# Attention and feed-forward block on one core: columns as operands, two operations on another engine, quarter loads together, another order

## What is computed

```python
x = x + _L0_xattn_ref(_layernorm(x), ctx, Wq, bq, Wk, bk)   # softmax((ctx Wq')(ctx Wk')'), mixes the 256 columns of x
x = x + _L0_ffn_ref(_layernorm(x), w_norm, w_gv, w_out)     # RMS norm, 8-bit rows, ternary weights, value * silu(gate)
...
x = x + _L1_xattn_ref(_layernorm(x), ctx, mask, Wq, Wk, Wv, Wo)   # 16 heads of 128, 8 key/value heads
x = x + _L1_ffn_ref(_layernorm(x), gate_w, up_w, down_w, scales)  # weights rounded to float8, silu(gate) * up
...
```

## Time and profile before

| | us |
|---|---|
| three timed runs | 310.63, 313.87, 313.88 |
| their median | 313.87 |
| the profiled execution | 312.58 |
| its span, first to last instruction | 310.5 |
| TensorE busy in the span | 293.6 |
| VectorE busy | 260.9 |
| ScalarE busy | 253.7 |
| GpSimd busy | 218.5 |

### The profile page before, as it was taken

How to read it: one execution, slowest core, us unless ns; L and a number is a source line. 1 busy time by engine, 2 the same in 40 slices (tenths; PEclk the granted TensorE clock), 3 DMA queues, 4 the chain that set the end, 5 groups by cost and what they waited for, 6 DMA issues and landing times.

```text
span 310.5 us, 6396 instructions
## 1 busy us (share of the span) xinstructions
PE 293.6 (95%) x1980; PEld 259.9 (84%) x1992; DVE 260.9 (84%) x713; ACT 253.7 (82%) x603; POOL 218.5 (70%) x290
## 2 busy tenths in 40 slices
PE   3968999999999999999999999999999999999994
PEld 2755487798989998979889999999988999899884
DVE  3959999999999999889999986997768897675665
ACT  2398995598999998979999899778899999855460
POOL 3558864556998578999879998886678798952001
PEclk9979999999999999999999999999999999999999
DMA  7996032001326548885878756537645647200103
GB/s 223 367 381 199 35 101 70 1 8 30 93 47 189 157 138 251 220 212 139 228 210 226 199 144 174 161 108 219 182 144 148 179 143 211 68 3 0 36 1 101
DMA packets 54609, 44.59 MB, mean 144 GB/s; under 512 B 11696, under 2 KB 45104, under 8 KB 54576
## 3 DMA queue, kind: packets, MB, share of 16 engines
q1 hardware_dynamic: 54016, 43.93, 49.0%
q10 hardware_dynamic: 560, 0.26, 0.3%
HBM read 27.01 MB, written 15.20 MB: 136 GB/s over the span
## 4 chain that ended last, share of the span: by engine, by line
PE 59%; DVE 20%; DMA 8%; issue 5%; SPq 4%; ACT 2%; DVEq 0%
PE pb L2016 41%; DMA block_room<-blocks 5%; PE pb L2279 5%; PE pb L2314 4%; DMA wraw<-in_wgvT 3%; DVE blocks L1581 3%; SPq L442 2%; DVE sm L1564 2%; PE pb L2130 2%; PE pb L2091 2%; PE pb L2076 2%; DVE wraw L1455 2%; DVE step L1601 1%; PE pb L2227 1%; DVE q_lo L1551 1%
## 5 line engine op out<-in xcount | busy, mean ns | idle before, releaser
L667 POOL TENSOR_TENSOR tp_lo<-tp,pT_hi 128x512 fp32r<-128x512 f32 x54 | 70.0, 1311 | 15.1 <-ACT pT_hi L993 14.8
L981 ACT ACTIVATE sm<-sm,smin 128x256 f32<-128x256 f32 x128 | 63.6, 501 | 4.7 <-DVE smin L1564 4.4
L1564 DVE CUSTOM_DVE_ANT_0 sm<-pb,mask_all 128x256 f32<-128x256 f32 x128 | 47.3, 418 | 5.6 <-PE pb L2016 5.5
L1581 DVE STREAM_TRANSPOSE blocks<-sm 128x1024 f32<-128x1024 f32 x27 | 33.5, 1240 | 7.4 <-DMA block_room<-blocks 7.0
L2016 PE MATMUL pb<-ctx_hi,q_hi 128*128 128x256 f32 x128 | 38.1, 298 | 1.1 <-DVE q_lo L1551 0.6
L662 POOL TENSOR_SCALAR sm<-sm,srec 128x256 f32<-128x256 f32 x64 | 30.5, 488 | 10.4 <-DVE srec L1570 10.4
L2016 PE MATMUL pb<-xT_hi,m_hi 128*128 128x256 f32 x128 | 37.3, 292 | 0.3 <-DVE xT_lo L1540 0.3
L2016 PE MATMUL pb<-n_hi,oT_hi 128*128 128x256 f32 x128 | 37.1, 290 | 0.2 <-DVE oT_lo L1595 0.2
L2016 PE MATMUL pb<-xT_hi,m_lo 128*128 128x256 f32 x128 | 36.2, 283 | 0.0
L2016 PE MATMUL pb<-xT_lo,m_hi 128*128 128x256 f32 x128 | 36.2, 283 | 0.0
L2016 PE MATMUL pb<-ctx_lo,q_hi 128*128 128x256 f32 x128 | 36.2, 282 | 0.0
(11 more groups left out here) (195 smaller groups left out, 943.0 us busy)
## 6 DMA issues: line engine op xcount, KB each, us to landing
block_room<-blocks SPq DMA_DIRECT2D x108, 128.0 KB, 2.8
tp<-block_room SPq DMA_DIRECT2D x54, 256.0 KB, 3.0
w_raw<-in_w SPq DMA_DIRECT2D x4, 576.0 KB, 4.6
wraw<-in_wgvT SPq DMA_DIRECT2D x4, 512.0 KB, 8.4
wraw<-in_woutT SPq DMA_DIRECT2D x2, 512.0 KB, 9.3
out<-xb SPq DMA_DIRECT2D x4, 256.0 KB, 2.2
xa<-in_x SPq DMA_DIRECT2D x3, 256.0 KB, 4.5
xb<-in_ctxT SPq DMA_DIRECT2D x2, 256.0 KB, 5.1
```

The source lines that it names most:

```text
L667: g.tensor_tensor(tp_lo[:, z, c, :], tp[:, z, c, :], as_f32(pT_hi[:, c, :]), ALU.subtract).then_inc(pT_lo_pool, 1)
L981: a.activation(sm[:, n % 2, k, :], sm[:, n % 2, k, :], ACT.Exp, bias=smin[:, n % 2, k:k + 1], scale=-1.0, accum_out=ssum[:, n % 2, k:k + 1 ...
L1564: v.tensor_tensor_reduce(out=sm[:, n % 2, k, :], in0=bank(passing_bank("s", 2 * n + h))[:, (k % 2) * S:(k % 2 + 1) * S], in1=mask_all[:, b ...
L1581: v.transpose(blocks[:].rearrange("p g k b -> p k g b"), sm[:, n % 2, :, :].rearrange("p k (g b) -> p k g b", b=32)).then_inc(blocks_done, 1)
```

## The change

1. GpSimd fills four columns of constants at the start (`minus_one`, `least`, `over_one`, `per_127`), and `nmean`, `ve` and `hstep` read them in place of numbers in the instruction. `hmax` and `hqs`, before one operation of two tensors each, are now one operation for each tile, with the deviation `rstd` as a column. VectorE's first statistics and GpSimd's first rows wait for 8 fills in place of 4.
2. `context_low` and the mask's values are GpSimd's. The mask's last column is no longer a maximum over the mask's bytes but a comparison of the first row minimum of each batch, made by VectorE in step n = 1, 9, 17 and 25, and `added3` waits for it.
3. The context's first half is the first load and its second half the sixth; the output weights' first piece goes behind the gate and value weights; `eighth(1)` to `eighth(3)` go out close behind `eighth(0)`.
4. `PASSING`, the banks of the sums, and the lists of calls of all five engines are new. What is computed of products is the same.

```diff
+        minus_one = tile(ctx, "minus_one", [P, 1])
+        least = tile(ctx, "least", [P, 1])
+        over_one = tile(ctx, "over_one", [P, 1])
+        per_127 = tile(ctx, "per_127", [P, 1])
...
+        SUMS, DOWN = 5, ((7, 4), (6, 5))
...
@@ -460,52 +464,54 @@
                     sp.wait_ge(fused_vo_ps, PAIRS)
                     sp.wait_ge(x1_done, B)
                     sp.wait_ge(wmean_done, 2)
-                    sp.wait_ge(mask_step, 2)
+                    sp.wait_ge(mask_step, 1)
                 four = slice(B * n * PIECE, B * (n + 1) * PIECE)
                 sp.dma_start(w8_raw[:, four], w8[:, four]).then_inc(ld_eight[n], 16)
 
+            contexts(0)
             projection(1)
             projection(0)
-            contexts(0)
             rows(1)
             rows(2)
+            contexts(1)
             rows(3)
             gate_value(0)
-            contexts(1)
             gate_value(2)
-            hidden_out(0)
             gate_value(1)
             gate_value(3)
+            hidden_out(0)
             hidden_out(1)
             raw(0)
...
             raw(3)
-            scales()
+            mask_bytes()
             raw(8)
             raw(2)
             turn_rows(1)
             raw(9)
-            mask_bytes()
             raw(7)
-            turn_rows(2)
             eighth(0)
             turn_hidden(2)
+            turn_rows(2)
+            eighth(1)
+            eighth(2)
             turn_hidden(3)
+            eighth(3)
             blocks_written(3)
-            turn_rows(3)
             blocks_read(3)
             blocks_written(4)
+            turn_rows(3)
             blocks_read(4)
             blocks_written(5)
             blocks_read(5)
             blocks_written(6)
             blocks_read(6)
             blocks_written(7)
-            eighth(1)
             blocks_read(7)
...
@@ -572,6 +576,10 @@
             g = nc.gpsimd
             g.memset(identf[:], 0.0).then_inc(ident_zero, 1)
             g.memset(nhalf[:], -0.5).then_inc(filled, 1)
+            g.memset(minus_one[:], -1.0).then_inc(filled, 1)
+            g.memset(least[:], EPS).then_inc(filled, 1)
+            g.memset(over_one[:], 1.0 + EPS).then_inc(filled, 1)
+            g.memset(per_127[:], 1.0 / 127.0).then_inc(filled, 1)
...
             def rows1(b):
                 if b == 0:
-                    pool.wait_ge(filled, 4)
+                    pool.wait_ge(filled, 8)
                 power(slice(0, 1), b, ve1_done, rstd1_done)
                 if b >= 2:
                     pool.wait_ge(xnT_ps, b - 1)
                 rows(xn[:, b % 2, :, :], xa, b, xn1_done)
+
+            def context_low(n):
+                pool.wait_ge(ctx_hi_done, n + 1)
+                g.tensor_tensor(ctx_lo[:, ctx_part(n)], ctx_raw[:, ctx_part(n)], as_f32(ctx_hi[:, ctx_part(n)]), ALU.subtract).then_inc(ctx_lo_done, 1)
+
+            def mask_values():
+                pool.wait_ge(ld_mask, 16)
+                g.tensor_scalar(mask_all[:, 0:B, 0:S], mask8[:], -MASKED, MASKED, ALU.mult, ALU.add).then_inc(mask_step, 1)
...
@@ -1386,10 +1405,6 @@
             v.memset(onesf[:], 1.0).then_inc(filled, 1)
             v.memset(plus_round[:], ROUND)
             v.memset(minus_round[:], -ROUND).then_inc(filled, 1)
-
-            def context_low(n):
-                dve.wait_ge(ctx_hi_done, n + 1)
-                v.tensor_tensor(ctx_lo[:, ctx_part(n)], ctx_raw[:, ctx_part(n)], as_f32(ctx_hi[:, ctx_part(n)]), ALU.subtract).then_inc(ctx_lo_done, 1)
 
             def values_low(c):
                 dve.wait_ge(cr_hi_done, c + 1)
@@ -1407,12 +1422,14 @@
                 for t in range(sl.start, sl.stop):
                     v.bn_aggr(mv[:, t, :], bnst[:, t, :]).then_inc(mv_done, 1)
                 dve.wait_ge(mv_done, bn_count[0])
-                v.tensor_scalar(nmean[:, sl], mv[:, sl, 0], -1.0, None, ALU.mult)
+                v.tensor_scalar(nmean[:, sl], mv[:, sl, 0], minus_one[:, 0:1], None, ALU.mult)
 
             def variances(sl, done):
-                v.tensor_scalar(ve[:, 0, sl], mv[:, sl, 1], EPS, None, ALU.add).then_inc(done, 1)
+                v.tensor_scalar(ve[:, 0, sl], mv[:, sl, 1], least[:, 0:1], None, ALU.add).then_inc(done, 1)
...
             def stats1(b):
+                if b == 0:
+                    dve.wait_ge(filled, 8)
...
-                v.tensor_scalar(ve[:, 0, sl], mv[:, sl, 1], EPS, None, ALU.add)
-                v.tensor_scalar(ve[:, 1, sl], mv[:, sl, 1], 1.0 + EPS, EPS * EPS, ALU.mult, ALU.add).then_inc(ve2_done, 1)
+                v.tensor_scalar(ve[:, 0, sl], mv[:, sl, 1], least[:, 0:1], None, ALU.add)
+                v.tensor_scalar(ve[:, 1, sl], mv[:, sl, 1], over_one[:, 0:1], EPS * EPS, ALU.mult, ALU.add).then_inc(ve2_done, 1)
...
-                scale_next(v.tensor_tensor(hmax[:, sl], hmax[:, sl], rstd[:, 1, sl], ALU.mult))
-                scale_next(v.tensor_scalar(hstep[:, sl], hmax[:, sl], EPS, 1.0 / 127.0, ALU.max, ALU.mult))
+                for t in range(sl.start, sl.stop):
+                    one = slice(t, t + 1)
+                    scale_part(v.tensor_scalar(hmax[:, one], hmax[:, one], rstd[:, 1, one], EPS, ALU.mult, ALU.max))
+                dve.wait_ge(scale_step, scale_count[0])
+                scale_next(v.tensor_scalar(hstep[:, sl], hmax[:, sl], per_127[:, 0:1], None, ALU.mult))
                 scale_next(v.reciprocal(hrec[:, sl], hstep[:, sl]))
-                scale_next(v.tensor_tensor(hqs[:, sl], hrec[:, sl], rstd[:, 1, sl], ALU.mult))
+                for t in range(sl.start, sl.stop):
+                    one = slice(t, t + 1)
+                    scale_part(v.tensor_scalar(hqs[:, one], hrec[:, one], rstd[:, 1, one], None, ALU.mult))
+                dve.wait_ge(scale_step, scale_count[0])
                 if b == 0:
                     dve.wait_ge(wmean_done, 1)
                 v.tensor_scalar(gsc[:, sl], hstep[:, sl], wmean[:, 0:1], None, ALU.mult).then_inc(gsc_done, 1)
...
-            def mask_values():
-                dve.wait_ge(ld_mask, 16)
-                v.tensor_reduce(mask_all[:, 0:B, S], mask8[:], AX.X, ALU.max).then_inc(mask_step, 1)
-                dve.wait_ge(mask_step, 1)
-                v.tensor_scalar(mask_all[:, 0:B, 0:S], mask8[:], -MASKED, MASKED, ALU.mult, ALU.add).then_inc(mask_step, 1)
...
                 if n == 0 and h == 0:
-                    dve.wait_ge(mask_step, 2)
+                    dve.wait_ge(mask_step, 1)
+                if n % PAIRS == 1 and h == 0:
+                    dve.wait_ge(sm_done, 4 * n)
+                    v.tensor_scalar(mask_all[:, b, S:S + 1], smin[:, 0, 0:1], 0.5 * MASKED, None, ALU.is_lt).then_inc(mask_step, 1)
...
             def added3(b):
                 dve.wait_ge(attn_ps, PAIRS * (b + 1))
+                dve.wait_ge(mask_step, b + 2)
```

1109 lines of the change are left out of this document (557 added, 552 removed), and 47 rows, old and new, of the table PASSING.

## The result

The changed kernel takes 314.93 us (median of 17 runs, 313.38 to 317.13), the kernel before 312.68 beside it (17 runs, 310.43 to 316.22). The ratio is **1.0073, 95% interval 1.0044 to 1.0103**. The forecast was 311.4 us, on the other side of no change. The profiled execution took 315.72 us, with a span of 313.9, 3.4 us more than before.

What follows compares the result with a forecast made beforehand. TensorE, busy for 293.6 of 310.5 us, was taken as the bound, with only its idle time and lower-clock cost to win. From the profiled 312.58 us, 0.6 and 0.6 were taken off to give 311.4 us; range 307.8 to 316.2.

Steps and rivals of the forecast that it cites:

- the slower rival: GpSimd becomes the bound ahead of the first hidden tile's integer rows and holds VectorE back: 314.9 us, chance 0.20.
- the prediction's own sign: Wrong if TensorE's idle time up to 60 us changes by over 1.5 us, or new holes appear behind 160.
- Step 1: Start of the kernel: context loaded first, so TensorE starts at about 4.6 us, 0.6 us earlier; bounds 0 and 0.93.
- Step 2: New order up to 40 us: two holes in place of one long one, counted 0; bounds 1.2 won, 2 lost.
- the faster rival: The holes close and TensorE's clock stays at 2.4 GHz around 15 to 18 us: 307.9 us, chance 0.18.
- Step 3: VectorE's small operations read columns, some one-wide: counted 0 on TensorE's path; bounds 0.8 won, 2.7 lost.
- Step 4: 3.85 us of work moved from VectorE to GpSimd: counted 0; bounds 0.4 won and the slower rival's loss.
- Step 5: Last weights' quarters loaded near 76 to 92 us, easing 120 to 160 us: 0.6 us won; bounds 0 and 1.4.

Runs made afterwards that it cites:

- e7: Kernel before with only the context's first part loaded ahead of the first part of x; ratio 0.9994.
- e1: Changed kernel with ScalarE's rounding of the context's first part, and so the table load, early again; ratio to the kernel before 1.0039.
- e5: e4 with the activation table load early again; ratio to the kernel before 1.0020.
- e6: Kernel before with only the activation table load made late, as in the changed kernel; ratio 0.9982.
- e11: Kernel before with only constants read from columns and the one-wide operations; ratio 1.0062.
- e15: Kernel before with only the one-wide operations, constants still numbers; ratio 0.9980.
- e3: Changed kernel with the context's low part and the mask values back on VectorE; ratio to the kernel before 1.0106.
- e4: Changed kernel with e2 and e3 together, leaving the order, first load and quarter loads; ratio to the kernel before 1.0042.
- e2: Changed kernel with numbers in place of columns and the two-wide product again; ratio to the kernel before 1.0061.
- e12: Kernel before with only the context's low part and the mask values moved to GpSimd; ratio 0.9999.
- e18: e16 with the context's low part and the mask values on GpSimd; ratio to the kernel before 1.0027.
- e16: e5 with GpSimd's splits of the fused output weights spread to later places; ratio to the kernel before 0.9954.
- e10: Changed kernel with the three later quarter loads put apart again among the blocks' copies; ratio to the kernel before 1.0115.
- e8: Kernel before with only the three later quarter loads issued together; ratio 1.0071.
- e17: Changed kernel with only GpSimd's splits of the fused output weights spread to later places; ratio to the kernel before 1.0110.

## Why the prediction was wrong

**The outcome against the text.** The sign was wrong: 0.8% faster was forecast, 0.7% slower came. A change within 1% had the largest chance, 0.53, and came, but the slower rival had only 0.20. By the prediction's own sign it was wrong too: TensorE's idle time up to 60 us grew by 2.6 us, from 10.2 to 12.8, where 1.5 was the limit.

**What held.** Little appeared behind 160 us (0.44 instead of 0.11 us of idle TensorE up to 200). GpSimd still waited ahead of `uq` (1.6 us in two waits), so it never became the bound there. Columns did not end the stretching, `hmax` and `hqs` were never over 215 ns, and the shortest `ve` and `nmean` took 214 and 228 ns. The slower rival had the time to the microsecond, 314.9, but that was luck: 1.0 us of it came from a wait that did not occur, the first load's 0.6 us were not won, and columns, order and table stood at nothing in it.

**Step 1, 0.6 us won: nothing.** It let the last weight land after the 2.9 us of the earlier trace rows, although the context, 256 KB, now went out ahead of it. It took 3.6 us (3.8 in e7), and TensorE began at 5.28.

**Step 2, order up to 40 us, counted 0: the first step that failed.** I walked ScalarE's list without the table load that its first activation brings. It stands in the changed kernel's instruction list, in front of the first copy; I did not look for it. It costs 0.2 to 0.3% in this order (e1, e5, each within overlapping intervals) and nothing in the old one (e6). Of the two holes of 2 us that the walk found, the one before energy(2) did not come, and the one before energy(3) was 0.96 us (at 20.08). No stretch at 1.2 GHz came behind it: the granted clock is 1.00 and the mix from 21.48 on takes 1.89 us, not the 3.40 of the earlier trace rows. That part of the faster rival came true, without making the kernel faster.

**Step 3, columns on VectorE, counted 0: the largest term that was mis-sized.** The durations at rest were right, and what e11 lost lies under the upper bound of 2.7 us. Wrong was the verdict that nothing of it lies on the path, in a text that says a few lines earlier that VectorE is full. e11 measures 0.62%, 1.9 us, e15 shows that none of it is the one-wide operations, and e3 against e4 gives 0.64% in the new order. Only e2 shows next to nothing, where GpSimd has the extra work. Wrong too was that what falls on `ve` and `nmean` "stays where it falls": the step added some 3.5 us to VectorE's small operations (2.7 + 1.6 - 0.8), and they grew by 6.9, from 12.1 to 19.0 us, of which the order brought 4.0 (e4). (The one-wide operations, 1.6 less 0.8 in the step, brought 0.5 in e15.)

**Step 4, GpSimd's share, counted 0.** True in the old order (e12, 0.9999). In the new one it depends on what the moved instruction meets: 0.7% of loss in e18 against e16, while with the columns in place it was, if anything, a gain (1.0073 against e3's 1.0106). VectorE lost 3.85 us of work and was as full as before, and the growth of its small operations is more than that. The price that the rival set on one such meeting, 0.75 us, was somewhat low: the moved low part took 0.94 from `nmean` (1.17 for 0.23), and the splits, which the rival did not name, 1.31 from the gate operations (2.19 for 0.88).

**Step 5, quarters, 0.6 us won: right in the view, wrong in the balance.** TensorE's idle time from 120 to 160 us did fall to 0.59, under 1 us, but in the new order it stays low with the quarters apart (e10). In the kernel before the quarters do win 0.9 us in this stretch and lose 2.0 in the one ahead of it, for 0.7% in all (e8). The step looked at the stretch that the loads leave and put no price on the one that they enter; its bounds, 0 and 1.4 won, had no loss.

**What the order costs by itself.** 0.2% (e5), and of that the place of GpSimd's splits beside VectorE is more than all: moved, the same order runs at 0.9954 (in the changed kernel as a whole the same move gained nothing, e17). I had looked at TensorE's holes and ScalarE's queue, and never laid GpSimd's new list beside VectorE's.

The parts do not add up exactly. Table 0.2 to 0.3%, columns 0.1 to 0.6%, GpSimd's share -0.3 to 0.7% and the order 0.2% are each known to about 0.4%, and they change with what else is there. That all of them push on one full engine, VectorE, fits this, but is argued and not shown by a run of its own. **Left open** is why e17 gained nothing in total. Its first 60 us were 2.8 us shorter than the changed kernel's, but its profile is of the shortest of its seven executions (313.59 us, the median is 315.60), and the changed kernel's of one above its median (315.72, 314.93), so the two profiles are no fair pair. Its small operations took 20.4 us, more than any other kernel's here.

## What to carry to other kernels

Where an engine is full, 60 ns on each of 40 small operations can cost more than half a percent (e11), so they are not to be counted as nothing. Moving work from VectorE to GpSimd did not pay here in any order with numbers as constants, and lost where GpSimd ran it beside VectorE's small and two-input operations (e18): lay both lists side by side before moving or reordering anything, sum the operations that can be held, and look for places where the other engine is idle or reads the accumulators. When an order changes, ask which instruction is now ScalarE's first activation: the table load goes with it. An edit that gains in one order can lose in another (the table, the quarters), so try it in the order in which it will stand.

## What the hardware showed that I had not expected

- A VectorE operation on 2 numbers per partition can take 1.17 us and ends within 0.02 us of the end of GpSimd's instruction beside it, whether its scalar is a number (e18) or a column (the changed kernel). GpSimd pays too: its conversion of 128x512 took 0.81 instead of 0.61 us beside the gate operation. What reads the matmul's accumulators was not held in the changed kernel, though the same subtractions of GpSimd run beside some of it:

```profile
L1529 DVE TENSOR_TENSOR m_lo<-pb,m_hi x8: 662/678/684, 48.7 to 90.5; 128x512 fp32r<-128x512 f32 x8
```

  The Trainium skill (SBUF — State Buffer, Who interferes with whom) gives the shared port to whoever comes first for the whole instruction, and exempts operations with one SBUF input outside the two-port modes. These runs agree in the ends (51.54 and 51.52 us). The prediction had this rule before it, and used it for the columns and not for the new order.
- The same eight products can take 3.78 us or 1.99 in kernels whose TensorE lists are the same. The first energies took 3.78 us from 9.62 on in the changed kernel, and in e4, behind the same eight products from 5.3 on, 1.99:

```profile
9.68 1.99 PE L2080 MATMUL pb<-qk 128*128 128x256 f32 x8 [0.57 <-ACT qk L902]
```

  3.78 us is also what the very first eight take in both, and 1.89 what eight of this shape take later on, so it looks like the lower and the upper level of TensorE's clock; but the granted clock reads 1.00 over both stretches, and the records do not settle it. e2 has the 3.78 as well, e3 the 1.99. As nothing on TensorE ahead of these products differs, I take the 1.8 us as no edit's doing. They are part of the 62.9 us of the changed kernel's query product and not of e4's 61.0, and one profile does not tell them from a cause.
